# Two attention stages of a recurrent block on one core: write weights sent earlier, and the output product B formed by batch in column groups

## The reference, cut to what matters

```
x0 = bi_wkv(x, fside, ...)                      # two scans per channel, exp, divide
for _ in range(2):
    logits = rms(x0, norm_pre) @ compete_w.T + compete_b       # T x S per batch
    vals, idx = top_k(logits.T, 4); wgt = softmax(vals)
    written = sum_k wgt_k * (x0[idx_k] @ write_w.T + write_b)  # S x C per batch
    ws = rms(ws + written, norm_post)
    kk, vv = ws @ wk.T + bk, ws @ wv.T + bv                    # S x C per batch
    att = softmax((x0 @ wq.T + bq) . kk * scale)  over the 16 slots, per head
    x0  = rms(x0 + (att @ vv) @ out_proj.T + ob, norm_post)
out = x + x0
```

## Time and profile before

| | |
|---|---|
| median of 3 runs | 1091.42 us (1088.33 to 1092.97) |
| the profiled execution, its own time | 1089.35 us |
| its span, first to last instruction | 1087.5 us |
| PE busy | 1016.5 us, 93% |
| DVE, ACT, POOL busy | 744.5, 592.4, 456.4 us |
| mean granted TensorE clock | 0.984 of full speed |
| DMA | 232.38 MB, mean 214 GB/s |

### The profile page before, as it was taken

One profiled execution on the slowest core, in us unless ns is written; L12 is line 12 of the kernel. 1 busy time (PEld: TensorE's weight loads), 2 busy tenths in 40 slices (PEclk: granted clock), 3 DMA queues, 4 the chain that ended last, 5 costly groups with the idle time before them and its releaser, 6 DMA issues. The chain is left out here.

```text
span 1087.5 us, 14367 instructions
## 1 busy us (share of the span) xinstructions
PE 1016.5 (93%) x4784; PEld 576.4 (53%) x4784; DVE 744.5 (68%) x1024; ACT 592.4 (54%) x977; POOL 456.4 (42%) x212
## 2 busy tenths in 40 slices
PE   2999999999999878989999999997899899999995
PEld 0444444444444424566666666665245666666663
DVE  5999999999999533645555555554335566666664
ACT  3888888888888601535555555556014323333323
POOL 7899999999999210001111111111100033333333
PEclk9999999999999989999999999999799999999998
DMA  4466565656564489844466575543898566868664
GB/s 141 154 187 200 181 207 176 211 171 215 168 215 153 134 325 378 282 155 176 174 222 212 188 237 192 178 157 136 315 382 272 189 216 234 291 228 295 220 228 154
DMA packets 122142, 232.38 MB, mean 214 GB/s; under 512 B 8162, under 2 KB 83042, under 8 KB 119012
## 3 DMA queue, kind: packets, MB, share of 16 engines
q1 hardware_dynamic: 121444, 229.54, 61.6%
q0 software_dynamic: 640, 2.10, 0.6%
HBM read 139.32 MB, written 92.28 MB: 213 GB/s over the span
## 5 line engine op out<-in xcount | busy, mean ns | idle before, releaser
L975 PE MATMUL bank<-work 128*128 128x256 f32 (+1 forms) x1024 | 244.4, 382 | 7.8 <-PEq L564 4.5
L1004 PE MATMUL bank<-work 128*128 128x512 f32 (+1 forms) x512 | 230.3, 592 | 2.1 <-ACT work L1106 1.3
L975 PEld LDWEIGHTS bank<-work 128*128 128x128 f32 x1024 | 187.2, 190 | 44.9 <-issue 25.0
L1166 POOL TENSOR_TENSOR work<-work 128x1024 f32<-128x1024 f32 x32 | 75.4, 2358 | 236.4 <-DVE work L1088 236.4
L1156 POOL COPY xres<-work 128x1024 f32<-128x1024 f32 x32 | 33.3, 1040 | 332.9 <-DVE work L1088 332.9
L424 PE MATMUL bank<-work,ident 128*128 128x512 f32 x256 | 126.9, 619 | 23.9 <-DVE work L339 22.8
L1004 PEld LDWEIGHTS bank<-work 128*128 128x128 f32 x512 | 97.1, 190 | 97.6 <-issue 91.8
L1039 DVE TENSOR_TENSOR work<-bank,sbias 128x256 f32<-128x256 f32 x64 | 27.2, 425 | 152.1 <-PE bank L975 152.1
L409 POOL TENSOR_TENSOR work<-work 128x1024 f32<-128x1024 f32 x32 | 85.2, 2661 | 22.9 <-ACT work L324 8.2
L403 POOL TENSOR_SCALAR work<-work 128x1024 f32<-128x1024 f32 x32 | 89.0, 2783 | 4.0 <-DMA work<-in_kT 1.3
L424 PE MATMUL bank<-work 128*128 128x511 f32 x192 | 90.4, 594 | 0.0
(11 more groups left out here) (161 smaller groups left out, 1607.1 us busy)
## 6 DMA issues: line engine op xcount, KB each, us to landing
work<-in_kT SPq DMA_DIRECT2D x32, 512.0 KB, 3.7
work<-in_xT SPq DMA_DIRECT2D x32, 512.0 KB, 3.9
x0T_scratch<-work SPq DMA_DIRECT2D x32, 512.0 KB, 3.2
x_natural_scratch<-xres SPq DMA_DIRECT2D x32, 512.0 KB, 5.1
work<-x0T_scratch SPq DMA_DIRECT2D x32, 512.0 KB, 4.4
x_natural_scratch<-work SPq DMA_DIRECT2D x32, 512.0 KB, 2.8
x1T_scratch<-work SPq DMA_DIRECT2D x32, 512.0 KB, 2.7
work<-x1T_scratch SPq DMA_DIRECT2D x32, 512.0 KB, 4.9
```

What stands on the lines that cost most here:

```text
L975: last = nc.tensor.matmul(ps_s[p], xTb[p][:, c, :], Amat[:, i, :, c * 32:c * 32 + 32], start=(c == 0), stop=(c == NC - 1))
L1004: last = nc.tensor.matmul(ps_o[:, cols], attT[:, k * P:(k + 1) * P], Bmat[k][:, i, cols], start=(k == 0), stop=(k == 1), skip_group_check= ...
L1166: nc.gpsimd.tensor_tensor(x1s[p], x1s[p], xo[p], ALU.add).then_inc(fin, 1)
```

## The change

It touches the two heads, the end of the recurrence and the end of tail 0.

1. Write pieces 0 and 1 are split into blocks of 512 KB (`first_piece`) and sent before the head: for head 0 near the end of the recurrence, for head 1 near the end of tail 0, each block as its place in `work` comes free. k piece 0 too goes early: at the very start of head 0, and within tail 0 for head 1.
2. The small loads (write bias, slots, norm weights, output bias) move behind the last gather.
3. Head 0's spread of the logits goes by quarter first, batch second. VectorE reads the logits from the bank; the bias is added to the four chosen values afterwards, and ScalarE's copy is gone.
4. Four more `keep_warm` matmuls, two after the first step of `Xb`, one after the second and one after the third.
5. Product B goes by group of one half k and one batch b (`groups`): 2 x 4 matmuls with 32 weight columns each, which fill one bank of 128 rows that is already the layout of `Bmat` and `stageB`. A group needs one copy: groups 0 to 3 on VectorE, which adds the bias, 4 to 7 on ScalarE. The one-row bias matmuls are gone. SP stores four groups, 512 KB each.
6. wo is sent by ScalarE's queue, as soon as TensorE has done with a pair of products. The score bias is copied in one instruction in place of two.

```diff
+        def first_piece(sp, slot, a):
+            w, i = ((wr_T, 0), (wr_T, 1), (wk_T, 0))[slot]
+            sp.dma_start(ring[slot][:, a, :], w[:, 4 * i + a, :]).then_inc(first_in[slot], 16)
...
+        groups = [(0, 2), (0, 0), (0, 1), (0, 3), (1, 2), (1, 3), (1, 0), (1, 1)]
...
-                    piece(0, wr_T, 0)
...
+                    if t == 0:
+                        for a in range(4):
+                            first_piece(sp, 2, a)
                     sp.wait_ge(g_in[K - 1], 16)
-                    piece(1, wr_T, 1)
-                    piece(2, wk_T, 0)
...
-                        for b in range(B):
-                            for q in range(Q):
+                        for q in range(Q):
+                            for b in range(B):
                                 last = nc.tensor.matmul(psB[32 * b:32 * b + 32, q * TQ:(q + 1) * TQ],
...
                     keep_warm(psX, 8)
+                    for k in range(1, K):
+                        pe.wait_ge(xb_ok, k)
+                        keep_warm(psX, 2 if k == 1 else 1)
...
+                    pe.wait_ge(vv_ok, 4)
+                    pe.wait_ge(sb_ok, 1)
+                    wait_product(pe, HP - 1)
+                    for g, (k, b) in enumerate(groups):
+                        if g % 4 == 0:
+                            for i in range(2):
+                                pe.wait_ge(wo_in[2 * k + i], 16)
+                        wait_group(pe, g - 3)
+                        for h in range(2):
+                            cols = slice(CH * h, CH * h + CH)
+                            for j in range(4):
+                                last = nc.tensor.matmul(group_bank(g)[32 * j:32 * j + 32, cols],
+                                                        vvz[:, 4 * k + j, b, :], ring[k][:, j, cols],
+                                                        start=True, stop=True, skip_group_check=True)
+                        last.then_inc(grp_ps, 1)
...
+                def group_home(eng, g):
+                    k, b = groups[g]
+                    eng.wait_ge(grp_ps, g + 1)
+                    if b < 2:
+                        if k == 0:
+                            for j in (2 * b, 2 * b + 1):
+                                eng.wait_ge(st_a[j], 16 * 2)
+                        return Bmat[k][:, b, :]
+                    if (k, b) == (0, 3):
+                        eng.wait_ge(b_out[t][0, 2], 16)
+                    if (k, b) == (1, 3):
+                        eng.wait_ge(b_out[t][0, 3], 16)
+                    return stageB[k, b]
...
+                        act.wait_ge(prod_ps, i + 2)
+                        act.dma_start(ring[i // 4][:, i % 4:i % 4 + 2, :], wo_T[:, i:i + 2, :])\
+                            .then_inc(wo_in[i // 2], 16)
+                    for g in range(4, 8):
+                        nc.scalar.activation(group_home(act, g), group_bank(g)[:, :], ACT.Copy).then_inc(grp_a, 1)
```

More of the change, by code:

```diff
@@ L712, in _ @@
-                    wait_product(pe, 2 * HP - 4)
-                    keep_warm(prod(2 * HP - 4), 3)
+                    for hp in range(HP):
+                        ps = prod(hp)
+                        wait_product(pe, hp - 2)
+                        if hp % 4 == 0:
+                            pe.wait_ge(w_in[hp // 4], 16 * 2)
+                        for c in range(NC):
+                            last = nc.tensor.matmul(ps[:, c * P:(c + 1) * P],
+                                                    ring[hp // 4][:, hp % 4, c * P:(c + 1) * P], kkz[:, hp, :, :],
+                                                    start=True, stop=True)
+                        last.then_inc(prod_ps, 1)
@@ L879, in wait_Bm @@
             def wait_Bm(eng):
-                for k in range(4):
-                    eng.wait_ge(b_out[t][k], 32 * (3, 3, 1, 1)[k])
+                for g in b_out[t]:
+                    eng.wait_ge(b_out[t][g], 16)
             ps_s = [banks[0][:, 0:256], banks[0][:, 512:768]]
@@ L951, in _ @@
                                     sp.dma_start(Bmat[part][:, i, :], Bm_d[b + 1, part, :, :]).then_inc(mat_in, 16)
+                            if first and b == B - 1 and tc == 4:
+                                wait(sp, o_ps, NC * (B - 1))
+                                first_piece(sp, 2, 0)
+                                first_piece(sp, 2, 1)
+                                first_piece(sp, 0, 0)
                             step(b, tc, b * NC + tc, tc % 2)
@@ L956, in _ @@
                     for m in range(NT - 4, NT):
+                        if first and m == NT - 2:
+                            wait(sp, sc_ps, NT)
+                            for slot in (2, 0):
+                                for a in (2, 3):
+                                    first_piece(sp, slot, a)
+                        if first and m == NT - 1:
+                            wait(sp, o_ps, NT)
+                            first_piece(sp, 0, 1)
+                            first_piece(sp, 1, 3)
                         store(m, m % 2)
@@ L960, in _ @@
                     if first:
+                        first_piece(sp, 1, 2)
+                        for p in range(2):
+                            wait(sp, xt_ps, NT - 1 + p)
+                            wait(sp, saved, NT - 1 + p)
+                            wait(sp, ssq2_ok, NT - 1 + p)
+                            sp.wait_ge(xn_out[1][p], 16 * NT // 2)
+                            first_piece(sp, 1, p)
                         sp.wait_ge(x1T_out, 16 * NT)
```

217 lines of the change are left out of this document (101 added, 116 removed).

## The result

The changed kernel took 1083.66 us (median of 6 runs, 1082.59 to 1089.83) against 1092.03 for the kernel before on the same chip (6 runs, 1088.33 to 1096.61). The ratio is 0.9937, with a 95% interval from 0.9919 to 0.9956: about 6.9 us less, where 18.6 were forecast. A second comparison on another chip gave 0.9914 (0.9884 to 0.9944), 9.4 us. The sign was right; between a third and a half of the forecast gain came, and the time lies outside the range of 1067 to 1082.

What follows compares the result with a forecast made beforehand. Heads were taken as bound by a serial opening, a DMA-paced middle and an end paced by copies out of the banks. Savings of 5.4 + 1.9 + 4.0 and 1.9 + 1.4 + 4.0, 18.6 us, gave 1073 us, range 1067 to 1082.

Steps and rivals of the forecast that it cites:

- the two ends: Product A's start to the tail's second row tile: 37.9 us against 42, 4.0 us saved in each head.
- elsewhere nothing: Recurrence's end and tail 0: the extra blocks sent there cost nothing, SP being ahead of what it waits for.
- the opening of head 0: Head 0's start to the end of its write projection: 5.4 us saved, between 2.2 and 6.
- the middle of head 1: Head 1, write projection to product A: waits for v pieces shrink to 0.8 us, saving 1.4 us.
- groups that don't run side by side: Rival, product B: a group takes 4.5 us instead of 1.82, 21 us more per head, 1116 us; chance 0.04.
- The opening of head 1: Head 1's start to the end of its write projection: 1.9 us saved, bounds 1 and 3.3.
- ScalarE's four DMA issues fall into its gaps: Heads' end, during product A: issuing wo from ScalarE fits between its half copies, product A unchanged at 14.46 us.
- the new gap is 1 to 2 us, so I take full clock: Head 0's opening: TensorE's short idle keeps full clock, so the projection takes 7.3 us and ends at 401.2.
- holds up only the first gathers: Head 0's opening: k piece 0, issued at 378.4, is in by 387 and delays no later gather.
- the clock: Rival, head 0's opening: low clock catches the four extra matmuls, 3.3 us gone, 1076 to 1078 us; chance 0.10.
- DMA keeps the pace: Rival, heads: transfers share engines worse, middle gains nothing, B's stores hold the second row tile: 1080 us; chance 0.10.
- the sends don't come early: Rival: SP reaches the blocks late, the write projection waits, only the end's 8 us stay: 1083 us; chance 0.04.

Runs made afterwards that it cites:

- Experiment 2: Changed kernel with the last write block sent behind the recurrence's last two stores and the other blocks sooner: 1085.14 us, ratio 0.9925 to the kernel before.
- Experiment 12: The kernel of experiment 8 with 11 instead of 8 matmuls without a reader at the start of head 0: 1077.05 us, ratio 0.9855 to the kernel before.
- experiment 1: The changed kernel run once more, no edit: 1084.46 us, ratio 0.9914 to the kernel before.
- experiment 8: Changed kernel with the edits of Experiment 2 and experiments 5, 6 and 7 together: 1079.74 us, ratio 0.9872 to the kernel before.
- experiment 9: Changed kernel without loading wo; product B multiplies by the q weights instead, so the result is not the reference's: 1078.79 us, ratio 0.9872 to the kernel before.
- experiment 7: Changed kernel with group 5 copied to a place of its own, not group 3's: 1084.46 us, ratio 0.9911 to the kernel before.
- experiment 3: Changed kernel with wo back on SyncE's queue, each piece behind a store of A: 1086.83 us, ratio 0.9932 to the kernel before.
- experiment 5: Changed kernel with TensorE waiting for product A's last copies only at group 2: 1086.2 us, ratio 0.9928 to the kernel before.
- experiment 6: Changed kernel with the second row tile's load waiting for one store of B, not four: 1081.6 us, ratio 0.9893 to the kernel before.
- experiment 10: The kernel of experiment 8 without the loads of wo, q weights in their place: 1074.95 us, ratio 0.9828 to the kernel before.
- experiment 11: Changed kernel with only the edits of experiments 5, 6 and 7, write blocks sent as in the changed kernel: 1081.59 us, ratio 0.9891 to the kernel before.
- experiment 4: Changed kernel with no write or k block sent ahead of a head: 1091.2 us, ratio 0.9985 to the kernel before.

## Why the prediction was wrong, step by step

In short: the forecast added up what each engine does and carried over how long the transfers take. Four terms failed by it: the two ends (4.0 each), "elsewhere nothing" (which lost 3.5 to 3.9), the opening of head 0 (5.4, of which 0.7 was left together with that late start) and the middle of head 1 (1.4, and 2.2 lost). The range was narrower than the working as well: its own lower bounds gave 1086, and 1067 to 1082 left that out. The measured 1083.66 lies inside the bounds.

**Right.** The sends come early (slices 14 and 28). The spread takes 1.93 us where TensorE comes to it at full clock (2.0 forecast), for 16 matmuls that took 4.57 in the old order. The write projections take 7.07 us in both heads (7.3 forecast). A group of product B is 1.74 us (13.94 for eight, forecast 1.82): the slower-side rival, groups that don't run side by side, is refuted. TensorE ends product B where I said, if it may start it. The opening of head 1 gave 2.8 and 2.9, of which the later end of tail 0 took 1.3 and 0.9 back.

**"ScalarE's four DMA issues fall into its gaps", and the end at 4.0 us per head: wrong.** I asked what the issue costs the engine that issues, and took the landing time of A's stores from the kernel before, where `wo` stood between them on one queue. The transfer was not in the sum. Four kernels show the landing of one 256 KB store of A in head 0 (medians of eight): 2.1 us without `wo`, 4.8 and 5.1 with it between the stores on the same queue, 7.5 with it on a second one. In all ten traces with `wo` on the second queue the median of a head is 5.6 to 8.6. The places of A are four, so VectorE's last copy waits (1.03 and 2.5 us), TensorE idles 2.66 and 4.11, and comes to product B at the low clock (15.58 and 16.91 us in place of 13.94). Then the second row tile, which is loaded when B's last store has landed, comes late with product B. The issues themselves did fit into ScalarE's gaps (0.33 to 0.40 us each, in gaps of 2.49). The kernel before did not mind since 24 copies of B, not the last copies of A, set its end, and product B did not wait for A's last copies there (it started at 14.29). The change took away the cover under which those stores were late. Measured size: 0.5 and -1.2 us in one execution, 1.0 and 1.4 in the other, against 4.0.

The Trainium skill ("DMA: Bandwidth & Descriptors", Queues, rings and completion order) says that a DMA engine goes round the queue rows that have work for it, a packet each. On one row a store waits only for what was queued ahead of it; with `wo` on another row it shares from its first packet. The 5.1 and 7.5 us agree with that, but as `wo` was also issued earlier in the second case, they do not show it by themselves. The prediction cited the same page for a bandwidth and not for this.

**"Elsewhere ... nothing": wrong at one place.** I worked out SyncE's issue time for the blocks and found SP ahead of what it waits for. I did not look at what stood behind them: a store that a barrier waits for. It cost head 0 a late start of 3.9 and 3.5 us, and through the longer idle the clock in the spread (3.47 us for 1.93). My check, average GB/s by slice (134 and 136), hides a burst: from 375 to 382 us the 16 engines were busy the whole time (in the kernel before, their share there was 0.80, at 259 GB/s).

```profile
375.00:382.00 7.00, 2.16 (x24) 1.27 (x24) 0.69 (x2) 2.97 (x4) 0.00 (x0) 1.00 1.04 369
```

At the end of tail 0 ScalarE's last copy to `x1T` waited 1.6 us for the store of `x1T_scratch` before it, which took 6.3 us where it took 2.7; there was no such wait in the kernel before. The marks lose 1.3 and 0.9 us there. I have not tested that one by itself.

**Opening of head 0, "the new gap is 1 to 2 us, so I take full clock": wrong.** Experiment 2 shows the term by itself, as the head starts on time there: the write projection ends 25.6 us after the start, 2.6 sooner than before and not 5.4. The gathers are issued 4.0 us sooner (3.7 forecast) and the weighted sum is complete at 392.5 (392.1 forecast). But the first gather, held up by the k piece and the last block, starts the extra matmuls, and the step "holds up only the first gathers" forgot that. The gap ahead of them is 2.80 us, and there the rival *the clock* came true: they run at the low level and stand in the way. That the changed kernel shows 4.6 and 4.2 for this line is luck: its late head let the traffic pass first. Experiment 12 closes the gap and gets 4.0 with a head that starts on time.

**Middle of head 1: 1.4 us forecast, 2.2 lost.** The write projection ended at 784.97. I had pieces following each other every 5.1 us, the second v piece landing 14.8 after that. The pieces ahead of it were in time (the first v piece landed 8.7 after it, 9.7 forecast), but the second landed at 801.83, 16.9 after: 8.1 us behind the first, where the kernel before shows 5.1. The windows around the landing of the first v piece say where the 3 us went, first the changed kernel, then the kernel before from 7.0 to 11.0 us behind its write projection, as in the second row:

```profile
784.00:792.00 8.00, 7.62 (x71) 2.59 (x67) 2.88 (x4) 1.19 (x4) 0.00 (x0) 1.00 1.00 428
792.00:796.00 4.00, 4.00 (x44) 1.30 (x40) 0.00 (x0) 0.69 (x1) 0.00 (x0) 1.00 0.89 303
796.00:804.00 8.00, 4.47 (x38) 1.22 (x30) 1.69 (x4) 0.00 (x0) 0.00 (x0) 0.90 0.99 418
```

```profile
795.60:799.60 4.00, 2.75 (x28) 0.68 (x24) 0.00 (x0) 0.69 (x1) 0.00 (x0) 1.00 1.02 426
```

The rate is close to that of the earlier trace rows on both sides and drops to 303 GB/s for some 4 us between. Experiments 1, 8 and 9 have the same dip in the same place (336, 279 and 336 GB/s). A piece is issued only when its place is free, and for the second v piece that is 6.0 us after the write projection, before and now. Before, the first v piece was still 4.8 us from landing then; now, with a k piece less in the head, it was 2.7 us from it. So the likely reason is that less was queued behind it; that is argued from these times and not tested. From 794.39 on SyncE also sends the q pieces, which are then under way together with the v piece; how much that adds is open.

A wait of 2.2 to 2.5 us (experiments 9, 2, 7 and 12) cost only itself, 27.5 to 27.9 us from the start of the write projection to product A. One of 2.6 (experiment 3) or of 3.0 to 3.6 us (experiments 1, 5, 6, 8, 10, 11 and the profiled execution) cost the clock as well, 29.6 to 30.7. The forecast's 0.8 us of waiting was too small by 1.4 to 2.8, and the clock added 1.7. Why the wait falls now on one side of that, now on the other, I can't say: the same instructions in head 1 gave 3.0 (experiment 8) and 2.2 (experiment 12).

**The rivals.** *DMA keeps the pace* (given 0.10) came nearest, with 1080 forecast and 1083.66 measured, except that it was not the middle and B's stores alone, but the stores of A and the barrier too. It deserved the larger chance, since three of my terms each leaned on DMA having room. Its argument against, "two 2 MB pieces more have left the head's middle", was true and did not help the ends. The 1083 of *the sends don't come early* is met by accident: the slices show that they did.

**What stays open.** Whether the dip in the middle of head 1 comes from the short queue. Whether A's stores are slower because of the second queue or because `wo` is issued sooner. And the size of single edits: their intervals are 0.5 to 0.7% wide, and of the edits alone none is told from the changed kernel by timing. The combinations (experiments 8, 10, 11 and 12) and the removal of `wo` are, against the first comparison (0.9919 to 0.9956); against that of experiment 1 (0.9884 to 0.9944) only 10 and 12 are.

## What to carry to other kernels

Moving a transfer to another queue gives it no bandwidth of its own: list what else is on the DMA engines in that stretch, and ask which of those transfers somebody waits for, first of all stores that free a buffer and stores ahead of a barrier. Send a prefetch behind the last such store, not ahead of it. Before sending something ahead of a chain of small transfers, ask what the first of them starts. And when a change removes the bound of a stretch, take none of the other durations there as given: they were measured under its cover, and the quickest test is to leave the suspected traffic out for one run.

## What the runs showed of the hardware

- The same 256 KB store from SBUF, medians of a head: 2.1 us with no weights on the way, 4.8 to 5.1 with megabyte reads between the stores on the same queue (one by one 2.1 to 8.8), 5.6 to 8.6 with those reads on a second queue, where they were also issued 1.7 us sooner.
- A 512 KB store behind seven 512 KB reads on its queue took 6.6 and 6.8 us, in place of 2.6.
- The idle time alone does not tell at which level of its clock (1.2 or 2.4 GHz) TensorE comes back. Where it was at the full clock before the idle, in the heads and their first row tiles of all fourteen traces, it kept it after every idle of up to 1.9 us and lost it after every one of 2.91 us or more. Between 1.97 and 2.90 both happened:

```profile
828.19 15.64 PE L716 MATMUL bank<-work 128*32 128x512 f32 x128 [1.97 <-issue]
467.23 1.97 PE L1032 MATMUL bank<-work 128*128 128x256 f32 x8 [2.90 <-DMA work<-x0T_scratch]
```

  The first row (experiment 4) is product B, 13.94 us at full clock, after the copies of product A; its granted clock was 0.57 in the first 4 us. The second (experiment 1) is a row tile at full pace, granted clock 1.00. An estimate of a wait of 2 to 3 us is an estimate with two outcomes.
- Losing the clock cost about the same whatever followed: 1.7 us for 8 records of the extra matmuls (5.40 for 3.70), for 32 of a projection (5.34 for 3.64), for 64 (8.77 for 7.07) and for 128 of product B (15.64 for 13.94). After an idle of 4.11 us it was 3.0 (16.91).
- A gather of 128 rows issued 3.7 us after the last of five 512 KB blocks landed in 6.0 us; issued 5.4 us after the last of four, it took 3.6.
